# A convolution in two blocks of 128 tokens, and layernorm statistics on ScalarE, in the first stage of a fused attention and FFN kernel

## The chip, the cores and the metric

The kernel runs on one core of one Trainium2 chip. The metric is the device time of one execution in microseconds. A profile of one execution is kept beside the times; its span (first to last instruction) is longer than the times of the unprofiled runs.

## The reference, cut to what matters

Four blocks run one after the other on x of shape (8, 256, 256) (batch, token, channel): an attention block with a state space model, a routed tree FFN, a second attention and a mixture of experts. The change lies in the first block, except that the statistics of its result, which the second block needs, are taken inside the first stage too. For each batch, with `layernorm` written as LN:

```python
x_text = LN(x)                                   # the input statistics
scores = (x_text @ Wq) . (ctx @ Wk) / sqrt(32)   # 4 heads, 256 x 256
topv, topi = top_k(scores, 32); probs = softmax(topv)
attn_mean = mean over heads of probs at topi, 0 elsewhere
c_t = attn_mean @ (ctx @ Wv)
x1 = LN(x_text) * g + b, scaled and shifted by c_t @ W_film_in
y  = irfft(rfft(x1, n=512) * rfft(K, n=512))[:256] + x1 * D_skip   # causal convolution
y  = y scaled and shifted by c_t @ W_film_out
xt = x_text + y
h  = gelu(LN(xt) @ W1 + b1) @ W2 + b2
x  = x + LN(xt + h)                              # then the second block takes LN(x)
```

The convolution kernel K (256 channels x 256 taps) comes from exp(dt*A) of 64 states and is computed once, before the loop over batches.

## The kernel before, in words

The work of the first stage (`first_stage`) is laid out on 128 partitions: a batch of 256 tokens is ST = 2 tiles of 128 tokens. The transforms are real matrices of sines and cosines at 256 half-odd frequencies, applied by TensorE. The stage has a prologue, in which VectorE builds the tables of the state space model (from the start to about 87 us), TensorE turns them into K and its spectrum `kr`, `ki`, and the first batches are projected; and a loop that is written out as steps i = -1 to 9. A step works on four or five batches at once: m = i (attention average, modulation, convolution), b = i+1 (top-32 selection), f = i+2 (input norm, projections, scores), e = i-1 (second layernorm and the FFN's products), z = i-2 (output norm and result). Each engine has its own `step(i)`, a fixed order of instructions; engines wait for each other by semaphores.

- VectorE (`dve`): `xt` of e and its statistics (L820, L821), `xr` of z and its statistics, then for b the first eight maxima of each of R = 8 rows (4 heads x 2 tiles, `eight`, L773) and their removal (`take`, L783), `x1` of m (L849, L853), `x_stats(i + 3)` and `next_stats(i - 3)` (L754, L879), three more rounds of maxima, then L866 subtracts the row maximum from the 32 selected values, four of the last eight removals, `shares_of` (L793: sums of the exponentials), the other four removals, and `pairs_of` (L805, L808), whose result `pair` TensorE needs first in the next step (L1195).
- ScalarE (`act`): copies from PSUM, `exponents` (L609), the copies of the modulation (L686), four gelus (L598), the copy of the spectrum `spec` (L693), four more gelus, `projected` (L615, L619), `top_exponents` (one instruction, L623), `scaled_shares` (L631), `scores_out` (L639). An ACT_TABLE_LOAD stands before the first gelu and before the first exponential after a gelu.
- GpSimd (`pool`): per batch rstd and offsets from VectorE's statistics (`factors`, `next_factors`, `root`), two full-size additions and products for z, `xt_pre` (L502), and the product of the two spectra (L508 to L517).
- TensorE (`pe`): transposes of `pair` (L1195), context product (L1209), `film_in` and `film_out` tiles (L1097), the first four of eight `up` chunks (L1106), the forward transform (L1240: 8 matmuls of 256 columns), the other four chunks, transposes and projection of f (L1125) between the two halves of `down` (L1118), scores (L1142, L1144), and the inverse transform (L1278: 8 matmuls of 256 columns).

A matmul in float32 stands as two records in the profile. `up(e)` writes four PSUM slots in turn, so that chunks 4 to 7 wait for the gelus of chunks 0 to 3. After the loop the next stage begins behind a barrier of all engines.

## Time and profile before

| | us |
|---|---|
| median of 3 runs (lowest, highest) | 1381.75 (1381.48, 1383.94) |
| span of the profiled execution, all that is recorded of its time | 1503.4 |
| first stage in the profile: prologue | 0 to about 118 |
| starts of VectorE's steps 1 to 8 (L820) | 155.23, 192.53, 229.85, 267.38, 304.99, 342.29, 379.54, 413.71 |
| last instruction of the first stage (L839) | 446.02 |
| busy share of the whole span: TensorE, VectorE, ScalarE, GpSimd | 80%, 59%, 39%, 31% |

How to read it: times in the rows are microseconds from the start of the profiled execution, and means are in ns where marked. A row of the timeline merges like instructions that stand next to each other (x16) and says in brackets how long the engine had been idle and what ended that. The clock of a window is the share of TensorE's full clock that was granted: 1.00 is 2.4 GHz, 0.50 is 1.2 GHz, and a value between them is a window with both.

### The profile page before, as it was taken

How to read it: one execution, taken by the hardware profiler on the slowest of the kernel's cores; microseconds unless marked ns; L12 is line 12 of the kernel's file. 1: busy time of each engine (PE TensorE's matmuls, PEld its weight loads, DVE VectorE, ACT ScalarE, POOL GpSimd, SP SyncE). 2: the span in 40 equal slices, each digit the busy share in tenths (PEclk: the TensorE clock that was granted, in tenths of full speed). 3: DMA queues.
4: the chain of work that ended last, by engine and by line, in shares of the span. 5: the costliest groups of instructions: out<-in, count | busy, mean ns of one | idle time of the engine just before them, and what ended most of it. 6: DMA issues, size and time to landing. Idle time of an engine off the chain costs nothing. (4 is left out here: it accounts for less than half of the span.)

```text
span 1503.4 us, 24492 instructions
## 1 busy us (share of the span) xinstructions
PE 1203.0 (80%) x7028; PEld 869.8 (58%) x7032; DVE 887.9 (59%) x2553; ACT 580.3 (39%) x1116; POOL 466.2 (31%) x749
## 2 busy tenths in 40 slices
PE   2597999999857756584958793868999989999997
PEld 1395677777646545373746672655666645555554
DVE  8998999999234643452625363565766634453534
ACT  2324566665322113252635331634666641212110
POOL 2237344555450336326141704622221000000000
PEclk9858999999979978697978896876999999999999
DMA  9000000000007412383823731625100000000000
GB/s 267 0 2 1 1 1 1 1 1 1 1 8 192 143 43 80 107 252 97 262 80 91 259 101 56 96 70 136 16 13 10 2 1 1 14 0 14 0 14 15
DMA packets 92463, 91.98 MB, mean 61 GB/s; under 512 B 27057, under 2 KB 77747, under 8 KB 92341
## 3 DMA queue, kind: packets, MB, share of 16 engines
q1 hardware_dynamic: 80052, 65.32, 14.5%
q0 software_dynamic: 12288, 25.18, 6.8%
q8 instruction: 59, 0.97, 0.3%
q14 instruction: 64, 0.52, 0.1%
HBM read 75.79 MB, written 14.68 MB: 60 GB/s over the span
## 5 line engine op out<-in xcount | busy, mean ns | idle before, releaser
L2263 PE MATMUL gq_psH<-gq_xT,gq_w 128*128 (+1 forms) x564 | 102.9, 309 | 53.3 <-ACT gq_act L1981 28.4
L2263 PEld LDWEIGHTS gq_psH<-gq_xT,gq_w 128*128 128x128 f32 x564 | 83.4, 209 | 81.6 <-issue 76.6
L3503 ACT ACTIVATE m_silu<-m_psG 128x512 f32<-128x512 f32 x48 | 28.7, 597 | 215.3 <-PE m_psU L3623 215.3
L2273 PE MATMUL gq_psY<-leaf_w,gq_hT 128*128 (+1 forms) x282 | 95.2, 422 | 20.0 <-issue 14.3
L3556 DVE TENSOR_TENSOR m_act<-m_silu,m_psU 128x512 f32<-128x512 f32 x48 | 33.0, 687 | 122.5 <-ACT m_silu L3503 107.7
L1865 POOL DMA_INDIRECT gq_x<-rows_x,gq_token_i x48 | 47.0, 979 | 174.0 <-PE gq_psX L2252 105.6
L3623 PE MATMUL m_psG<-m_xnT,m_gate 128*128 128x512 f32 x192 | 91.2, 597 | 2.1 <-PEq L192 2.1
L3623 PE MATMUL m_psU<-m_xnT,m_up 128*128 128x512 f32 x192 | 91.4, 599 | 0.0
L2149 DVE SCALAR_TENSOR_TENSOR gq_hT<-gq_xT,unit_leaf,gq_act 128x128 f32<-128x128 f32 x141 | 49.6, 352 | 61.7 <-issue 28.6
L1981 ACT ACTIVATE gq_act<-gq_psH,leaf_b 128x128 f32<-128x128 f32 x141 | 51.4, 365 | 75.4 <-remote 41.5
L783 DVE MATCH_REPLACE8 s_product_a_rest<-a_top,s_product_a_rest 128x256 f32<-128x256 f32 x192 | 76.1, 408 | 0.3 <-issue 0.3
L3034 DVE TENSOR_REDUCE c_max<-c_psA 128x4 f32<-128x1024 f32 x32 | 39.2, 1226 | 61.3 <-PE c_psA L3185 61.3
L205 POOL TENSOR_SCALAR m_rstd<-m_mean_var 128x4 f32<-128x4 f32 x4 | 0.9, 232 | 229.8 <-DVE m_mean_var L1348 229.8
L2910 ACT ACTIVATE c_probT<-c_psA 128x2048 f32<-128x2048 f32 x32 | 60.1, 1878 | 28.5 <-PE c_psA L3216 28.5
L2168 DVE TENSOR_TENSOR gq_y<-gq_psY,gq_y 128x256 f32 (+1 forms) x94 | 39.7, 422 | 46.9 <-remote 29.0
L3635 PE MATMUL m_psD<-m_down,m_act 128*128 128x256 f32 x256 | 60.9, 381 | 7.1 <-DVE m_acc L3581 7.1
L3581 DVE SCALAR_TENSOR_TENSOR m_acc<-m_psD,m_weight,m_acc 128x256 f32<-128x256 f32 x128 | 53.1, 477 | 22.3 <-PE m_psD L3635 22.3
L773 DVE MAX8 a_top<-s_product_a_rest 128x8 f32<-128x256 f32 x192 | 64.9, 410 | 2.0 <-DVE s_product_a_rest L783 0.5
L3623 PEld LDWEIGHTS m_psU<-m_xnT,m_up 128*128 128x128 f32 x192 | 37.1, 193 | 46.8 <-issue 46.8
L1106 PE MATMUL a_psW<-s_tables_a_work,a_w 128*128 128x256 f32 x256 | 60.8, 393 | 2.7 <-ACT s_tables_a_work L675 2.7
L3635 PEld LDWEIGHTS m_psD<-m_down,m_act 128*128 128x128 f32 x256 | 48.1, 190 | 25.6 <-issue 14.2
L1657 PE MATMUL gq_psH<-rows_ahead,gq_xT 128*128 128x256 f32 (+1 forms) x192 | 53.9, 429 | 9.3 <-ACT rows_ahead L1564 7.8
(574 smaller groups left out, 3063.6 us busy)
## 6 DMA issues: line engine op xcount, KB each, us to landing
leaf_w<-in_group_w SPq DMA_DIRECT2D x128, 128.0 KB
leaf_w<-in_group_w SPq DMA_DIRECT2D x64, 256.0 KB
a_w<-in_L_xattn_W SPq DMA_DIRECT2D x2, 1024.0 KB, 11.9
rows_x<-token_rows SPq DMA_DIRECT2D x8, 256.0 KB, 5.4
sorted_y_q<-gq_y SPq DMA_DIRECT2D x16, 128.0 KB, 3.9
sorted_y_k<-rows_ahead SPq DMA_DIRECT2D x16, 128.0 KB, 4.4
sorted_y_v<-gq_y SPq DMA_DIRECT2D x16, 128.0 KB, 1.7
rows_f<-token_rows SPq DMA_DIRECT2D x8, 256.0 KB
```

The source lines that it names most:

```text
L773: do.mark(dve.max(top[:, j, 8 * r:8 * r + 8], row_in(r, j)))
L783: last = dve.match_replace(rest[:, j, :], top[:, j, 8 * r:8 * r + 8], row_in(r, j), NEG_TAKEN)
L1106: last = pe.matmul(pW[:, 2 + c // 2 % 2, c % 2, :], w1[:, k, c * P:(c + 1) * P], hT[:, k, :], start=(k == 0), stop=(k == DC - 1))
L1657: last = pe.matmul(self.psL[n % 2][0:k, c, :], self.nw[:, f, d, c * P:c * P + k], self.xnT[:, b, d, :], start=(d == 0), stop=(d == DC - 1))
L1981: act.activation(act_h[n % 2][:], psH[n % 2][:, 0:P], ACT.Gelu if gelu else ACT.Relu, bias=weights.b1[:, first + f, bass.ds(g, 1)]).then_i ...
L2149: dve.scalar_tensor_tensor(hT[n % 2][:], xT[:, DC, bass.ds(g * -P + u * P, P)], leaves.unit_leaf[:, bass.ds(g, 1)], act_h[n % 2][:], ALU.i ...
L2263: last = pe.matmul(psH[n % 2][:, 0:P], w1[n % 3][:, c, :], xT[:, c, bass.ds(g * -P + u * P, P)], start=(c == 0), stop=(c == DC - 1))
L2273: pe.matmul(psY[n % 3][:, 0:D], hT[n % 2][:], weights.w2[:, bass.ds(g * D, D)], start=True, stop=True).then_inc(y_ps, 1)
L2910: act.activation(probT[c][:], psA[:], ACT.Exp, scale=float(DH1) ** -0.5).then_inc(exps.s, 1)
L3581: last = dve.scalar_tensor_tensor(acc[:, t, :], psD[:, t, :], wt[:, t, e:e + 1], acc[:, t, :], ALU.mult, ALU.add)
L3623: last = pe.matmul(o[u % 2][:], w[:, u, c, :], xnT[:, c, :], start=(c == 0), stop=(c == DC - 1))
L3635: last = pe.matmul(psD[:, t, :], act_u[u % 2][:, t * P:(t + 1) * P], down[:, u, :], start=True, stop=True)
```

## The change

It does four things, all in the first stage.

1. Convolution by blocks. The 256 tokens are two blocks of 128, and the transform has 128 frequencies (every second row or column of the old tables; for the inverse, the first 128 rows of the table, every second column, copied by GpSimd once). Both blocks are transformed at once, by two matmuls of 512 columns. The kernel's spectrum is kept for its first 128 taps (`kr[:, 0]`, `ki[:, 0]`) and for taps 128 to 255 (`[:, 1]`); `shifted_spectrum` combines them once with a sign per frequency, so that the second block's result is its own product plus the first block's product with the combined one. GpSimd multiplies in `block_products`: 4 products and 2 sums of 512 columns, signalled as `y_first`, then 4 products, 2 sums and 2 additions of 256 columns, signalled as `y_sb`. The inverse has 2 matmuls of 256 columns for each token tile.
2. Order. TensorE's forward transform now stands before all eight `up` chunks, and ScalarE copies the spectrum before all eight gelus.
3. Statistics. Mean and variance of x are taken by ScalarE (`sums`, `squares`, each with an accumulating output, for tiles 0-1, 2-3 and 4-15), all in the prologue; the small factors follow on GpSimd in the same three groups. The next stage's statistics, one batch a step before, are taken by VectorE for batches 0 to 4 in step 7 behind `x1`, and for 5 and 6 in step 9; GpSimd's factors follow in `next_factors(0, 5)`, at the end of step 7, and `next_factors(5, 7)`, in step 9.
4. Top-32 exponentials. L866 goes. ScalarE takes exp(scale * top - scale * max) in 8 instructions of 32 columns with the bias from `nmax`, and its table is loaded as before ahead of the first.

```diff
 # loads: half-length tables, cut by the DMAs; the kernel's table in 16 DMAs into a blanked tile
-        load(dft[:], self.dram["dft"], self.late)
-        load(idft[:], self.dram["idft"], self.late)
+        even = self.dram["dft"].rearrange("(p two) t k f -> two t p k f", two=2)
+        for t in range(ST):
+            load(dft[t * P // ST:(t + 1) * P // ST], even[0, t, :, :, 0:P], self.late)
+        load(idft_in[:], self.dram["idft"][:, 0], self.late)
...
 # gpsimd, step(i)
-                    if ST <= i + 3 < B:
-                        factors(i + 3)
-                    if 0 <= i - 4 < NEXT - 2:
-                        next_factors(i - 4)
                     if has(m):
                         reached(pool, fout_sb, m)
                         pool.tensor_tensor(f_out[:, :, D:2 * D], f_out[:, :, D:2 * D],
                                            xn[m % SLOTS][:], ALU.add).then_inc(xt_pre.s, 1)
+                        if m == 0:
+                            shifted_spectrum()
                         reached(pool, spec_sb, m)
...
+                        block_products(m)
+                    if m == B - 1:
+                        next_factors(0, NEXT - 2)
...
+                def block_products(m):
...
+                    for n, (a, k) in enumerate(four):
+                        do.mark(pool.tensor_tensor(part[n], x[a], own[k], ALU.mult))
+                    released(pool, y_ps, m)
+                    do.wait()
+                    do(pool.tensor_tensor(y[0], part[0], part[1], ALU.subtract))
+                    pool.tensor_tensor(y[1], part[2], part[3], ALU.add).then_inc(y_first.s, 1)
+                    reached(pool, y_first, m)
+                    for n, (a, k) in enumerate(four):
+                        do.mark(pool.tensor_tensor(part[n][:, 0], x[a][:, 0], shifted[k], ALU.mult))
+                    do.wait()
+                    do.mark(pool.tensor_tensor(part[0][:, 0], part[0][:, 0], part[1][:, 0],
+                                               ALU.subtract))
+                    do(pool.tensor_tensor(part[2][:, 0], part[2][:, 0], part[3][:, 0], ALU.add))
+                    do(pool.tensor_tensor(y[0][:, 1], y[0][:, 1], part[0][:, 0], ALU.add))
+                    pool.tensor_tensor(y[1][:, 1], y[1][:, 1], part[2][:, 0], ALU.add
+                                       ).then_inc(y_sb.s, 1)
...
 # scalar
                 def top_exponents(b):
                     reached(act, ranked, b)
-                    act.activation(etop[:], etop[:], ACT.Exp, scale=scale
-                                   ).then_inc(etop_sb.s, 1)
+                    for j in range(R):
+                        last = act.activation(etop[:, j, :], top[:, j, :], ACT.Exp,
+                                              bias=nmax[:, j:j + 1], scale=scale)
+                    last.then_inc(etop_sb.s, 1)
...
-                    if has(e):
-                        gelus(e, range(HC // 2))
                     if has(m):
                         reached(act, spec_ps, m)
                         released(act, y_sb, m)
                         act.activation(spec[:], pW[:, 0:2].rearrange("p c k d -> p c (k d)"),
                                        ACT.Copy).then_inc(spec_sb.s, 1)
                     if has(e):
-                        gelus(e, range(HC // 2, HC))
+                        gelus(e, range(HC))
...
 # vector, step(i)
                     if z == B - 1:
-                        next_stats(NEXT - 1)
+                        next_stats(NEXT - 2, NEXT)
...
-                    if ST <= i + 3 < B:
-                        x_stats(i + 3)
-                    if 0 <= i - 3 < NEXT - 1:
-                        next_stats(i - 3)
+                    if m == B - 1:
+                        next_stats(0, NEXT - 2)
...
-                        dve.tensor_tensor(etop[:], top[:], top[:, :, 0].unsqueeze(2)
-                                          .to_broadcast([P, R, TOPK]), ALU.subtract
-                                          ).then_inc(ranked.s, 1)
+                        reached(dve, ranked, b)
...
 # tensor, step(i)
-                    if has(e):
-                        reached(pe, hT_sb, e)
-                        up(e, range(HC // 2))
                     if has(m):
                         reached(pe, x1_sb, m)
                         for part in range(2):
-                            for k in range(2):
-                                for t in range(ST):
-                                    last = pe.matmul(pW[:, part, k, :],
-                                                     dft[:, t, part, k * P:(k + 1) * P],
-                                                     x1[:, t, :], start=(t == 0),
-                                                     stop=(t == ST - 1))
+                            last = pe.matmul(flat(pW[:, part]), dft[:, part],
+                                             x1[:].rearrange("p t d -> p (t d)"), start=True,
+                                             stop=True)
                         last.then_inc(spec_ps.s, 1)
                     if has(e):
-                        up(e, range(HC // 2, HC))
+                        reached(pe, hT_sb, e)
+                        up(e, range(HC))
...
                         for t in range(ST):
+                            reached(pe, (y_first, y_sb)[t], m)
                             for part in range(2):
-                                for k in range(2):
-                                    last = pe.matmul(pA[:, t, :],
-                                                     idft[:, k, part, t * P:(t + 1) * P],
-                                                     yspec[:, part, k * D:(k + 1) * D],
-                                                     start=(part == 0 and k == 0),
-                                                     stop=(part == 1 and k == 1))
+                                last = pe.matmul(pA[:, t, :], idft[:, part],
+                                                 yspec[:, part, t * D:(t + 1) * D],
+                                                 start=(part == 0), stop=(part == 1))
```

## Rows read from the trace of the kernel before

**Rows 1.** The page's first line: the span of the profiled execution.

```profile
span 1503.4 us, 24492 instructions
```

**Rows 2.** Stage windows, 215 to 260 us: busy us (instructions) by engine, clock, DMA.

```profile
215.00:260.00 45.00, 43.23 (x219) 33.64 (x218) 42.95 (x156) 26.27 (x50) 24.74 (x34) 1.00 0.00 1
```

**Rows 3.** Timeline of loop step 5: start us, us, engine, line, operation [idle before].

```profile
304.99 0.68 DVE L820 TENSOR_TENSOR s_tables_a_work<-a_psA,s_tables_a_work 128x512 f32<-128x512 f32 x1
318.01 2.32 PE L1106 MATMUL a_psW<-s_tables_a_work,a_w 128*128 128x256 f32 x10
320.94 1.28 ACT L598 ACT_TABLE_LOAD   x1
321.47 3.62 PE L1240 MATMUL a_psW<-s_tables_a_work,a_dft 128*128 128x256 f32 x16
322.24 1.57 ACT L598 ACTIVATE s_tables_a_work<-a_psW,a_b 128x256 f32<-128x256 f32 x4
...
332.38 1.03 PE L1125 MATMUL a_psB<-a_xnT,a_wq 128*128 128x256 f32 x4
333.16 0.89 DVE L866 TENSOR_TENSOR s_dC_a_etop<-a_top 128x256 f32<-128x256 f32 x1
333.44 0.38 ACT L619 ACTIVATE a_qk<-a_psB 128x256 f32<-128x256 f32 x1 [3.54 <-PE a_psB L1125]
335.14 0.42 ACT L623 ACTIVATE s_dC_a_etop<-s_dC_a_etop 128x256 f32<-128x256 f32 x1
335.59 0.42 DVE L793 TENSOR_REDUCE a_einv<-s_dC_a_etop 128x8 f32<-128x256 f32 x1
...
342.29 0.68 DVE L820 TENSOR_TENSOR s_tables_a_work<-a_psA,s_tables_a_work 128x512 f32<-128x512 f32 x1
342.52 2.02 PE L1195 MATMUL a_psW<-identity,s_Z_re_a_pair 128*128 128x128 f32 x16 [0.68 <-DVE s_Z_re_a_pair L808]
```

**Rows 4.** Timeline, VectorE: the two sets of statistics in step 3; where step 4 starts.

```profile
241.62 0.75 DVE L754 BATCH_NORM_STATS2 a_x_stats<-x_tokens 128x6 f32<-128x256 f32 x2
...
243.63 2.68 DVE L773 MAX8 a_top<-s_product_a_rest 128x8 f32<-128x256 f32 x8
...
267.38 0.68 DVE L820 TENSOR_TENSOR s_tables_a_work<-a_psA,s_tables_a_work 128x512 f32<-128x512 f32 x1
```

**Rows 5.** Groups by form, ScalarE: busy us, mean ns of one | idle before.

```profile
L609 ACT ACTIVATE s_product_a_prob<-a_score,a_nmax 128x256 f32<-128x256 f32 x64 | 26.4, 501 | 24.4 <-DVE a_nmax L776 24.4
...
L3496 ACT ACTIVATE m_score<-m_score 128x32 f32<-128x32 f32 x4 | 0.9, 229 | 0.9 <-DVE m_score L3516 0.9
```

**Rows 6.** Timeline, TensorE: matmuls that end pauses of 2.69, 3.33 and 3.34 us.

```profile
51.91 0.66 PE L1054 MATMUL a_psA<-identity,a_xn 128*128 128x128 f32 x4 [2.69 <-ACT a_xn L590]
...
379.76 0.46 PE L1195 MATMUL a_psW<-identity,s_Z_re_a_pair 128*128 128x128 f32 x2 [3.33 <-DVE s_Z_re_a_pair L808]
...
856.84 1.11 PE L2613 MATMUL t_psY<-identity,token_rows 128*128 128x128 f32 x4 [3.34 <-issue]
```

**Rows 7.** Stage windows around those pauses, and after the restart at 147.14 us.

```profile
51.00:57.00 6.00, 4.41 (x14) 3.45 (x15) 5.55 (x18) 2.19 (x5) 0.00 (x0) 0.73 0.01 3
377.00:383.00 6.00, 2.50 (x18) 2.27 (x19) 5.52 (x10) 0.62 (x2) 0.59 (x2) 1.00 0.00 0
855.00:861.00 6.00, 3.01 (x16) 2.54 (x16) 1.73 (x4) 1.28 (x2) 4.82 (x10) 0.57 0.57 127
...
147.00:152.00 5.00, 4.86 (x12) 3.89 (x13) 4.66 (x21) 3.00 (x8) 0.09 (x1) 0.50 0.00 0
```

**Rows 8.** Groups by form, GpSimd: busy us, mean ns of one | idle before.

```profile
L508 POOL TENSOR_TENSOR s_tables_a_work<-s_tables_a_work,kernel_re 128x512 f32<-128x512 f32 x8 | 10.2, 1271 | 24.2 <-ACT s_tables_a_work L693 24.2
...
L206 POOL TENSOR_TENSOR a_next_hold<-a_next_hold,minus_half 128x2 f32<-128x2 f32 x7 | 5.0, 710 | 0.6
...
L206 POOL TENSOR_TENSOR m_rstd<-m_rstd,m_minus_half 128x4 f32<-128x4 f32 x4 | 4.1, 1032 | 0.3
```

**Rows 9.** Timeline, GpSimd: the first factor of the last batch's second layernorm.

```profile
416.51 0.22 POOL L205 TENSOR_SCALAR a_rstd<-a_mean_var 128x2 f32<-128x2 f32 x1 [7.98 <-DVE a_mean_var L757]
```

More of the change, by code:

```diff
@@ L372, in has, with tiles_of @@
             return 0 <= n < B
+        def tiles_of(group):
+            return slice(*(ST * b for b in ((0, 1), (1, 2), (2, B))[group]))
         STEPS = range(-2, B + 2)
@@ L428, in film_gains, with next_factors @@
+                def next_factors(first, end):
+                    reached_apart(pool, n_var, end - 1)
+                    q = slice(first * ST, end * ST)
+                    n = q.stop - q.start
+                    do(standard_factors(core, pool, do, tokens.factor[:, q], n_hold[:, 0:n],
+                                        tokens.mv[:, q, 1], [h[:, 0:n] for h in n_half]))
                 def film_gains():
@@ L485, in step @@
                             biased.then_inc(last_biased, 1)
[L486 to L487 removed]
+                            next_factors(NEXT - 2, NEXT)
                         released(pool, o_sb, z)
@@ L534, in _ @@
                 pool.tensor_copy(neg_mask[:], neg_mask[:]).then_inc(picked, 1)
-                factors(0)
-                factors(1)
+                for n, value in enumerate((-0.5, 0.5)):
+                    do(pool.memset(n_half[n][:], value))
+                for group in range(3):
+                    centres(group)
+                    factors(group)
                 pool.wait_ge(tables, 2)
@@ L719, in _ @@
                 projected(0)
+                act.wait_ge(core.loads[0], 16)
+                sums(1)
                 scores_out(0)
+                squares(1)
                 film_folded()
-                act.wait_ge(core.loads[0], 16)
                 x_normal(1)
@@ L727, in _ @@
                     keys_out(n)
+                sums(2)
+                squares(2)
                 exponents(0)
```

184 lines of the change are left out of this document (117 added, 67 removed).

## The prediction

> **What bounds the kernel now.** I read first the windows over the loop, then the timeline of one step, then who ends each wait. In the loop TensorE is busy 43.2 of 45 us and VectorE 43.0, at full clock [rows 2]: neither alone sets the pace. Step 5 shows how they share it. VectorE starts it at 304.99 and the next at 342.29, 37.30 us later [rows 3]. Counted from the start: TensorE begins the first `up` chunks at 13.02, the projection ends in ScalarE's copy at 28.45, behind that stands a table load of 1.28, the exponential of the 32 selected values starts at 30.15, and VectorE's `shares_of` starts at 30.60, at once after its end (30.57). VectorE itself would have been ready earlier: L866 starts at 28.17, and 0.43 for it and 1.6 for four removals (0.4 each) give 30.2. So in a step with one set of statistics the chain TensorE, `projected`, table load, exponential sets `shares_of`, and everything behind it (6.70 us to the next start) hangs on that. Step 4, which has two sets, takes 37.61 (267.38 to 304.99) [rows 3, 4]: 1.0 us more of VectorE's work stretched it by only 0.31. VectorE's chain and the other one are within half a microsecond of each other. Shortening one alone is worth little.
>
> **The change, part by part, in one loop step with all its parts (steps 1 to 5).**
> VectorE loses one or two sets of statistics, 2.01 for two [rows 4], so 1.0 each, and L866 at 0.43 (0.89 where it meets GpSimd [rows 3]). It would be ready for `shares_of` at about 28.7.
> TensorE: 256 columns are two records of 0.216, 0.43 per matmul, from 16 records in 3.46 (321.47 less 318.01). The forward transform falls from 8 matmuls to 2 of 512 columns, 3.46 to 1.73; the inverse from 8 to 4, also 3.46 to 1.73. But the forward one now stands ahead of all `up` chunks, and these wait on gelus. From 13.02: transform to 14.75, chunks 0 to 3 to 18.21. ScalarE is done with its copies at 15.95 (where the load stands, 320.94), copies the spectrum for 1.02, loads the table for 1.28 (18.25), and two gelus of 0.37 to 0.47 end at 19.09 [rows 3]. Chunk 4 waits for them, so TensorE stands for 0.95 us; its last chunk ends at 22.65 where it ended at 23.40. Of 1.73 us it gains 0.75 before the projection (bounds 0.4, were the handshakes slower, and 1.73 without the stall). `x1` is ready before the transform needs it (in step 3, which starts at 229.85, VectorE is through with it at 241.62 [rows 4], 11.8 into the step) and costs nothing.
> ScalarE: one instruction of 0.42 becomes eight of 32 columns with a bias from a tile. None such is in the trace. The nearest: 32 columns without such a bias take 229 ns, 256 columns with it 501 ns [rows 5] and without it 0.42 [rows 3]. So the bias costs 0.08 and one of the eight takes 0.31. In a row they start before the last has ended, the 256-column ones by 0.10 (64 of them are 26.4 us busy, 0.41 each, for a mean of 501 ns [rows 5]), which leaves 0.21: 7 x 0.21 + 0.31 = 1.78, bounds 1.2 and 2.5 (eight times 0.31, no overlap). That is 1.36 more, on the chain that sets `shares_of`.
> Together `shares_of` starts at 30.60 - 0.75 + 1.36 = 31.2, 0.6 later than now, and VectorE, ready at 28.7, waits for it 2.5 us. Steps 1 to 5 take 37.9 each, 189.5 for 187.1 now: +2.4. The other four removals and `pairs_of` follow as before.
> GpSimd: 4 products and 2 sums of 512 columns at 1.27, 1.23 apart [rows 8], are 7.6 as before; the 8 operations of 256 columns add 6.0 at about 0.7 (bounds 0.64, half of 1.27, and 1.27). It starts behind the copy of the spectrum at 17.0, so `y_sb` is up at 30.6; TensorE comes to the second half of the inverse at 33.3. Hidden, with 2.7 to spare; at 1.27 per operation 2 us would stick out of it.
>
> **Prologue and step 0.** There VectorE paces nearly all. It loses two sets (1.0 each) and L866, and half of a third set (its first one hid partly behind ScalarE's sines), and gains 0.3 for two small operations on one column: -1.1 to the tables, -2.5 to the end of step -1, where 0.9 is given back because `top_exponents` stands before ScalarE's copy of the kernel. Step 0 loses a set and L866 and keeps VectorE as its pace. Step 1 then starts 1.95 earlier (bounds 1 and 3). ScalarE takes 16 sums and 16 squares, at 0.5 and perhaps 0.2 more for reading the accumulator. The 24 of the last group, some 17 us, have ScalarE's longest idle stretch to themselves, 24.4 us before the first L609 [rows 5]; were it gone, every one would push step -1 by 0.7. The 8 others stand in shorter idle stretches. The 16 small DMAs of the kernel's table are last in SP's queue and needed only after all of VectorE's tables; all the loads move fewer bytes.
>
> **Steps 6 and 7 and the end.** Step 6 has no projection, so the exponentials start when the maxima are done: 1.8 us less. Step 7 waits for the convolution alone: transform from 13.0, spectrum at 16.0, `y_first` at 23.6, `y_sb` at 29.6, inverse to 30.75, where it is now 34.2. But GpSimd, before it takes the layernorm factors of the last batch, now runs `next_factors(0, 5)` on 10 columns. A power on 2 columns is 0.71 and on 4 is 1.03 [rows 8], 0.16 a column, so 2.0 for 10. The factors of one batch, three powers, six small operations of 0.2 and their waits, are 4.3; on 10 columns 8.2 (bounds 4.3, were a power's time fixed, and 13, were it proportional). It ends at 37.8, and the factors that now start at 416.51, 36.97 into the step [rows 9] (step 7 starts 0.22 before the matmul at 379.76 [rows 6]), start 0.9 later. Up to here the sum is -1.95 + 2.4 - 1.8 + 0.9 = -0.5: nothing.
>
> **TensorE's clock.** Now 0.68 us pass between the last inverse matmul and the next step's first matmul [rows 3]. After the change it is 0.68 + 0.75 (it is earlier) + 1.73 (shorter inverse) + 0.6 (`pair` is later) = 3.76 us in every step. What such a pause does is in the trace. Seven pauses of 2.69 to 3.37 us began at full clock; six were followed by half clock. The first (clock 0.73 in 51 to 57), the last (0.57 in 855 to 861) and the one that kept 1.00, of 3.33 at 379.76, stand in [rows 6, 7]. All eight longer ones that began so were followed by half clock. So I take it that nearly every step begins at 1.2 GHz. What that costs: matmuls take twice as long until the clock returns, and after the pause that ended at 147.14 it was still at 0.50 five microseconds on [rows 7]. The step's beginning (transposes 2.0, context product 1.9, `film_in` 3.4) is broken by two copies, and lies on the path to the projection. I take 3.3 us a step (bounds 0 and 5.7, all of it up to most of `film_in` at half speed). 1.0 of this comes back, since the stall at chunk 4 goes when TensorE is late: 2.3 net. Step 1 2.5, steps 2 to 5 9.2, step 6 2.3, and step 7, with no stall to lose, 3.3: +17.3. The pause does not heal, because both its ends hang on the same projection.
> The Trainium skill, TensorE: Matmul & The Clock Gate, section "HAM oscillation — how this bites in real kernels", says that waits between short bursts send the array back to half rate each time, so that each burst starts cold. The trace agrees in 14 of its 15 pauses of over 2.6 us; by the rule the sum is the +17 above, by the one row that held it is about 0.
>
> **Sum.** -0.5 + 17.3 = +16.8 us on the profiled execution's span of 1503.4 [rows 1], the only time it has. The median of the runs is 1381.75, 121.65 less; the stage moves almost no data, so I carry the difference over one to one: 1398.6. In proportion it would be 15.4.
>
> **Rivals.**
> Clock holds (0.22): pauses come out shorter or the steps' phase spares them. For it: the pause of 3.33 that held, and an exponential nearer 1.2 us would leave 3.2. Against it: six of seven. The parts cancel: 1381, from 1376 (no stall at chunk 4, 1 us off in each of five steps) to 1387 (two steps of seven start cold).
> VectorE is the pace after all (0.16), and the time goes below that of before: the eight exponentials hide, `shares_of` starts at about 28.7, which needs the projection 1.5 us earlier and the exponentials at 0.1 us each. Steps 1 to 5 then save 1.9 to 2.2 each, and with -1.95, -1.8 and +0.9 the time is 1369. It decides as soon as the chain through ScalarE ends before VectorE's fourth removal. Against it: step 4 stretched by only 0.31 for 1.0 of VectorE's work.
> Slower by more than the forecast (0.06): GpSimd's 256-column operations take 1.0 or more and push the inverse, or the powers grow faster than 0.16 a column: 1407 and above.
>
> **How the numbers follow.** Forecast 0.56, with a range of its own from 1389 to 1406. The 8 in 10 range goes from 1374, which leaves most of the VectorE rival out, to 1407. A difference of 0.2% is 2.8 us. Slower by more than that: forecast 0.56, the last rival 0.06 and 0.06 of the clock rival, 0.68. Within: 0.11 of the clock rival, with 0.01 of the others, 0.12. Faster: 0.16 and 0.04 of the clock rival, 0.20.
>
> **What would show it.** Steps 1 to 5 of 39 to 42 us, clock below 1.00 in most of them, pauses before L1195's successor of 3.4 us or more; eight exponentials in 1.6 to 2.0; VectorE idle before `shares_of`; TensorE idle about 1 us inside the `up` chunks in steps that start warm; a gap of 4 us between `next_stats`' factors and the last layernorm. Full clock through the loop, or `shares_of` starting before 29.5, would make it wrong.

## The result, and the profile after

The changed kernel takes 1389.53 us in the median of 8 runs (1382.60 to 1399.45), the kernel before 1382.85 beside it: ratio 1.0068, 95% interval 1.0043 to 1.0094, in which one slow run of the kernel before, 1622.98, does not count. Run again later in 12 runs, unaltered, it took 1387.20 (1382.03 to 1399.54) against 1381.30: 1.0047, 1.0024 to 1.0071. So it is slower, by 6 to 7 us between the medians, where 16.8 was forecast; the sign, the mechanism and the range held, and the size was off by more than a factor of two.

One thing has to be known to read the profiles. The profiled execution of the changed kernel is its slowest, 1399.45, and its first stage (to the start of the last sum into x) ends at 463.29 us. In the kernel before that is 446.02, so there the stage is 17.3 us longer. The profiled execution of the later 12 ends it at 458.06. From that point to the end of the span the profiled executions of all kernels with the unchanged rest need 925 to 937 us, the unusual one of the kernel before excepted (1057). Stages are therefore compared by the trace, kernels by their medians.

The windows of the changed kernel's steps 1 to 7, from one of VectorE's starts (L916, the L820 of before) to the next; columns: window, its length, busy us (instructions) of TensorE, its weight loads, VectorE, ScalarE, GpSimd, the granted clock, DMA (the first line is the profile page's own):

```profile
span 1397.7 us, 24202 instructions
...
153.96:193.59 39.63, 34.37 (x158) 25.02 (x158) 32.06 (x113) 23.25 (x49) 15.76 (x19) 0.93 0.00 1
193.59:233.75 40.16, 34.91 (x158) 25.37 (x158) 33.63 (x118) 24.24 (x51) 20.87 (x26) 0.92 0.00 1
233.75:273.06 39.31, 33.75 (x158) 24.49 (x158) 33.63 (x118) 24.13 (x51) 20.87 (x26) 0.96 0.00 1
273.06:312.21 39.15, 33.90 (x158) 24.36 (x158) 33.61 (x118) 24.24 (x51) 20.88 (x26) 0.95 0.00 1
312.21:351.55 39.34, 33.77 (x158) 24.52 (x158) 33.62 (x119) 24.13 (x51) 20.89 (x26) 0.96 0.00 1
351.55:392.46 40.91, 35.20 (x122) 23.46 (x122) 34.17 (x118) 20.25 (x45) 20.87 (x26) 0.83 0.00 1
392.46:428.19 35.73, 33.50 (x122) 22.93 (x122) 9.56 (x36) 10.91 (x20) 22.53 (x28) 0.86 0.00 1
```

The reader is to see that no step has full clock, and that TensorE and VectorE are busy for only 34 of 39 us where it was 43 of 45 us [rows 2]: the change made both lighter and the loop slower. Step 5 of it, in a timeline, shows why; it answers to [rows 3], with the rows picked out that matter here:

```profile
312.21 0.68 DVE L916 TENSOR_TENSOR s_tables_a_work<-a_psA,s_tables_a_work 128x512 f32<-128x512 f32 x1
312.44 3.44 PE L1285 MATMUL a_psW<-identity,s_Z_re_a_pair 128*128 128x128 f32 x16 [3.79 <-DVE s_Z_re_a_pair L904]
326.66 1.88 PE L1325 MATMUL a_psW<-s_tables_a_work,a_dft 128*128 128x512 f32 x4
332.68 3.72 PE L1196 MATMUL a_psW<-s_tables_a_work,a_w 128*128 128x256 f32 x16 [0.68 <-ACT s_tables_a_work L685]
341.31 0.38 ACT L706 ACTIVATE a_qk<-a_psB 128x256 f32<-128x256 f32 x1 [3.54 <-PE a_psB L1215]
341.71 1.28 ACT L711 ACT_TABLE_LOAD   x1
343.00 1.80 ACT L711 ACTIVATE s_dC_a_etop<-a_top,a_nmax 128x32 f32<-128x32 f32 x8
344.84 0.42 DVE L889 TENSOR_REDUCE a_einv<-s_dC_a_etop 128x8 f32<-128x256 f32 x1 [3.61 <-ACT s_dC_a_etop L711]
345.98 2.00 PE L1364 MATMUL a_psA<-s_tables_a_work,a_idft 128*128 128x256 f32 x8
351.55 0.68 DVE L916 TENSOR_TENSOR s_tables_a_work<-a_psA,s_tables_a_work 128x512 f32<-128x512 f32 x1
351.78 2.67 PE L1285 MATMUL a_psW<-identity,s_Z_re_a_pair 128*128 128x128 f32 x16 [3.80 <-DVE s_Z_re_a_pair L904]
```

TensorE waits 3.79 us for `pair`; VectorE waits 3.61 us for the eight exponentials; they wait for the copy of the projection, and that waits for TensorE. The two engines wait for each other in turn. The 16 transposes behind the pause take 3.44 us, and 2.02 at full clock [rows 3].

### The profile page after: what moved, and what is told of

Its sections match the earlier page's. It is cut to its first block and busy times, and to the rows that moved or that the text cites. A ratio compares the mean times of both kernels' runs of the same rounds, so it can differ in the third digit from the quotient of the medians.

```text
span 1397.7 us, 24202 instructions
## 1 busy us (share of the span) xinstructions
PE 1174.1 (84%) x6872; PEld 835.4 (60%) x6872; DVE 877.6 (63%) x2515; ACT 610.2 (44%) x1242; POOL 497.2 (36%) x732
## 5 line engine op out<-in xcount | busy, mean ns | idle before, releaser
L2348 PE MATMUL gq_psH<-gq_xT,gq_w 128*128 (+1 forms) x564 | 98.8, 300 | 4.8 <-ACT gq_w L2058 2.6
L2348 PEld LDWEIGHTS gq_psH<-gq_xT,gq_w 128*128 128x128 f32 x564 | 78.8, 199 | 30.6 <-issue 25.9
L2358 PE MATMUL gq_psY<-leaf_w,gq_hT 128*128 (+1 forms) x282 | 89.5, 401 | 7.2 <-DVE gq_hT L2234 6.9
L2066 ACT ACTIVATE gq_act<-gq_psH,leaf_b 128x128 f32<-128x128 f32 x141 | 51.3, 364 | 37.9 <-PE gq_psH L2348 23.7
L3720 PEld LDWEIGHTS m_psD<-m_down,m_act 128*128 128x128 f32 x256 | 48.1, 190 | 25.6 <-issue 14.2
L1196 PEld LDWEIGHTS a_psW<-s_tables_a_work,a_w 128*128 128x128 f32 x256 | 49.2, 195 | 20.1 <-ACT s_tables_a_work L685 7.3
L2058 ACT ACTIVATE gq_w<-leaf_w 128x256 f32 (+1 forms) x141 | 58.3, 414 | 3.8 <-issue 3.7
```

Of the source, the lines that this page charges most:

```text
L1196: last = pe.matmul(pW[:, 2 + c // 2 % 2, c % 2, :], w1[:, k, c * P:(c + 1) * P], hT[:, k, :], start=(k == 0), stop=(k == DC - 1))
L2058: act.activation(w1[n % 3][:], weights.w1[:, :, bass.ds(g * P, P)], ACT.Copy).then_inc(w_sb, 1)
L2066: act.activation(act_h[n % 2][:], psH[n % 2][:, 0:P], ACT.Gelu if gelu else ACT.Relu, bias=weights.b1[:, first + f, bass.ds(g, 1)]).then_i ...
L2348: last = pe.matmul(psH[n % 2][:, 0:P], w1[n % 3][:, c, :], xT[:, c, bass.ds(g * -P + u * P, P)], start=(c == 0), stop=(c == DC - 1))
L2358: pe.matmul(psY[n % 3][:, 0:D], hT[n % 2][:], weights.w2[:, bass.ds(g * D, D)], start=True, stop=True).then_inc(y_ps, 1)
L3720: last = pe.matmul(psD[:, t, :], act_u[u % 2][:, t * P:(t + 1) * P], down[:, u, :], start=True, stop=True)
```

## The experiments

All were timed in five rounds against the kernel before, whose median was 1381.3 us (beside experiment 8: 1379.9). Each differs from the kernel named by its edit alone, of which the core is quoted. Each expectation sets two theories, A and B, against each other.

**1. The clock alone.** Changed kernel, TensorE kept busy in its pauses.

```diff
 # tensor, step(i), behind the inverse transform
+                    if 1 <= m <= B - 2:
+                        reached(pe, fout_sb, m)
+                        for _ in range(4):
+                            pe.matmul(flat(pC[:]), w1[:, 0, 0:P], w1[:, 0, 0:2 * S], start=True, stop=True)
```

> The changed kernel with four matmuls of 512 columns of which nothing is kept, issued by TensorE behind the inverse transform of batches 1 to 6, where it pauses for 3.8 us (3.45 us of work at full clock). Theory A (the pauses bring the half clock and that costs time): full clock from step 1 to step 6; the half-clock stretches at 192, 233, 274, 312, 353 and 394 us go; shares_of starts 31.2 to 31.6 us into a step instead of 32.6, steps of 38.1 us instead of 39.3; 6 to 10 us less than the changed kernel, 1380 to 1384, and a narrower spread of its runs. Theory B (the loop is slower by the exponentials alone, TensorE's half clock is covered by waits): no difference, 1389.

Measured: 1381.78, ratio 0.9986 (0.9962 to 1.0010). Its windows of steps 2, 5, 6 and 7:

```profile
194.42:232.33 37.91, 35.78 (x166) 24.60 (x166) 33.53 (x118) 24.25 (x51) 20.89 (x26) 1.00 0.00 1
...
308.17:346.08 37.91, 35.78 (x166) 24.61 (x166) 33.53 (x119) 24.25 (x51) 20.89 (x26) 1.00 0.00 1
346.08:381.92 35.84, 32.73 (x130) 22.33 (x130) 33.64 (x119) 20.36 (x45) 20.91 (x26) 1.00 0.00 1
381.92:413.44 31.52, 29.30 (x122) 20.80 (x122) 9.55 (x36) 11.02 (x20) 22.53 (x28) 1.00 0.00 1
```

TensorE has 3.5 us more work at full clock in each step, and steps 2 to 5 are 1.2 to 2.4 us shorter. Theory A. Without the half clock the change can't be told from the kernel before. 1387.20 less 1381.78 makes the clock 5.4 us in the medians; the two ratios, 1.0047 and 0.9986, make it 8.4, so its size is known only roughly.

**2. One exponential for the eight.** Changed kernel with VectorE's subtraction and ScalarE's single instruction of 256 columns put back.

```diff
 # scalar, top_exponents
-                    for j in range(R):
-                        last = act.activation(etop[:, j, :], top[:, j, :], ACT.Exp, bias=nmax[:, j:j + 1], scale=scale)
+                    act.activation(etop[:], etop[:], ACT.Exp, scale=scale)
```

> The changed kernel with VectorE's subtraction and the single exponential of 256 columns as before, all else changed. Theory A (ScalarE's chain of projection, table load and exponentials sets shares_of): 1.38 us less in each of steps 1 to 5, 0.43 more in steps -1 and 0, so -6; TensorE's pauses shrink from 3.8 to 2.4 us. If half clock still follows them 1383; if it does not, 1375 to 1378. Theory B (VectorE is the pace, or GpSimd's y_sb): 0 to +3, 1389 to 1392.

Measured: 1378.69, ratio 0.9980 (0.9962 to 0.9998), 8.5 us less than the changed kernel. The loss goes this way too, since the eight exponentials are what makes the pauses long. Steps with full clock take 36.5 to 37.0 us, and `shares_of` starts at 29.8 in them. The pauses are 2.40 to 2.90 us, and after three of five of them the clock stayed. The first of these rows held, the second fell (timeline of TensorE, then the windows from there):

```profile
192.58 2.02 PE L1284 MATMUL a_psW<-identity,s_Z_re_a_pair 128*128 128x128 f32 x16 [2.88 <-DVE s_Z_re_a_pair L899]
...
266.12 3.65 PE L1284 MATMUL a_psW<-identity,s_Z_re_a_pair 128*128 128x128 f32 x16 [2.88 <-DVE s_Z_re_a_pair L899]
...
192.00:197.00 5.00, 4.02 (x28) 3.43 (x28) 4.58 (x14) 0.98 (x2) 1.61 (x5) 1.00 0.00 0
265.00:271.00 6.00, 4.48 (x23) 4.25 (x24) 5.58 (x15) 1.12 (x3) 2.07 (x5) 0.72 0.02 4
```

**3. The eight exponentials on the kernel before**, and no other part of the change.

```diff
 # vector: behind the last maxima
-                        dve.tensor_tensor(etop[:], top[:], ..., ALU.subtract).then_inc(ranked.s, 1)
 # scalar, top_exponents
-                    act.activation(etop[:], etop[:], ACT.Exp, scale=scale)
+                    for j in range(R):
+                        last = act.activation(etop[:, j, :], top[:, j, :], ACT.Exp, bias=nmax[:, j:j + 1], scale=scale)
```

> The kernel before with only its exponentials of the selected values changed: no subtraction on VectorE, eight instructions of 32 columns on ScalarE. Theory A: the eight take 1.8 us for 0.42, shares_of starts 1.4 us later in each of steps 1 to 5 (31.9 to 32.0 us into a step), 0.43 us less in steps -1 and 0; TensorE's pause becomes 2.1 us and the clock stays; +6, 1387 to 1390. Theory B (VectorE is the pace of the kernel before): 0.4 less per step, 1379 to 1381.

Measured: 1390.04, ratio 1.0052 (1.0027 to 1.0078): 8.7 us more, the same as their price in the changed kernel. `shares_of` starts at 31.99 to 32.00 in steps with full clock, and after two of the five pauses of 2.07 us at the ends of steps 1 to 5 half clock followed, which the expectation had excluded. ScalarE and VectorE in step 4, which starts at 272.96 and has full clock:

```profile
301.83 1.28 ACT L624 ACT_TABLE_LOAD   x1
303.12 1.81 ACT L624 ACTIVATE s_dC_a_etop<-a_top,a_nmax 128x32 f32<-128x32 f32 x8
304.96 0.42 DVE L799 TENSOR_REDUCE a_einv<-s_dC_a_etop 128x8 f32<-128x256 f32 x1 [1.16 <-ACT s_dC_a_etop L624]
```

**4. The exponentials off the path.** Changed kernel, eight exponentials ahead of the copy of the projection.

```diff
 # scalar, projected(f): between the copy of xnT and the copy of the projection
+                    act.activation(warm[:], nmax[:, 0:1], ACT.Exp, scale=scale)   # loads the table
+                    top_exponents(b)
                     reached(act, proj_ps, f)
```

> The changed kernel with ScalarE's eight exponentials of the selected values ahead of the copy of the projection, and the table asked for by an exponential of one column that waits for nothing. Theory A (both ends of TensorE's pause hang on the chain projection, table load, exponentials): that chain leaves shares_of, which starts when VectorE's removals end, 29.0 to 29.4 us into a step instead of 32.6; the pause at the end of a step shrinks to under 1 us; full clock through the loop; steps 1 to 5 of 35.7 to 36.5 us; 1362 to 1370. Theory B (the exponentials only wait for VectorE's last maxima, and the copy of the projection, now behind them, delays the scores and with them TensorE): steps of 38 us or more, 1380 to 1389.

Measured: 1370.68, ratio 0.9909 (0.9876 to 0.9943) in 6 runs, just over the expected range; theory A, though the pause did not fall under 1 us as expected. Step 4 of it, ScalarE, VectorE and the end:

```profile
284.06 1.28 ACT L712 ACT_TABLE_LOAD   x1
285.36 0.20 ACT L712 ACTIVATE a_warm<-a_nmax 128x1 f32<-128x1 f32 x1
286.75 1.81 ACT L717 ACTIVATE s_dC_a_etop<-a_top,a_nmax 128x32 f32<-128x32 f32 x8 [1.19 <-DVE a_top L876]
288.46 0.36 ACT L709 ACTIVATE a_qk<-a_psB 128x256 f32<-128x256 f32 x1
288.58 0.42 DVE L900 TENSOR_REDUCE a_einv<-s_dC_a_etop 128x8 f32<-128x256 f32 x1 [0.17 <-ACT s_dC_a_etop L717]
...
295.51 2.02 PE L1296 MATMUL a_psW<-identity,s_Z_re_a_pair 128*128 128x128 f32 x16 [1.26 <-DVE s_Z_re_a_pair L915]
```

VectorE waits 0.17 us, not 3.61, and TensorE 1.26, not 3.79. The clock stays at full in steps 1 to 6, and steps 2 to 4 take 35.4 to 35.5. Nothing was made faster: 16 us of the changed kernel's median went by the order of two waits on ScalarE.

**5. The same order in the kernel before.**

```diff
 # scalar, projected(f): before the wait for the projection
+                    act.activation(warm[:], nmax[:, 0:1], ACT.Exp, scale=scale)
+                    top_exponents(b)                                              # one instruction
```

> The kernel before with its one exponential of the selected values, and its table load, ahead of the copy of the projection; all else as before. Theory A (in the kernel before, VectorE's own chain is half a microsecond behind the chain through ScalarE): shares_of starts at 30.2 us into a step with one set of statistics instead of 30.6, and at 31.2 in one with two sets; 2 us less in all, 1378 to 1381. Theory B (the chain through ScalarE was the only limit): shares_of at 29, 1372 or less.

Measured: 1380.79, ratio 1.0005 (0.9987 to 1.0022). Steps 1 to 5 take 36.89, 36.80, 37.51, 37.60 and 37.26 where they took 37.30, 37.32, 37.53, 37.61 and 37.30 [rows 3, 4]. Theory A: the kernel before had VectorE's chain right behind the other, so the order alone is worth 1 us there in all five, and the medians can't be told apart. The slack that experiment 4 uses is what the change made.

**6. The changed kernel once more.**

```diff
 # no line differs
```

> The changed kernel itself, unaltered, beside the others of this job. Theory A (each step starts behind a pause of 3.8 us and at half clock, and how long the half clock lasts after it differs from one execution to the next): pauses of 3.8 us again, half-clock stretches at other places and of other lengths than in the first profile, runs spread over more than 8 us, median 1386 to 1391. Theory B (the cost per step is fixed): runs within 4 us of each other.

Measured: 1387.20, runs from 1382.03 to 1399.54. Six pauses of 3.75 to 3.80, all followed by half clock again, for 3.4 us four times and for 6.8 twice; in the first profile it was 3.4 three times, and 6.8, 13.7 and 10.2. So the length differs between executions, as theory A has it. The spread of the times, 17 us, proves less than I expected of it: the kernel before ranges over 11 beside it and over 15 in all runs of the experiments (1373.88 to 1389.49), and it had full clock in its loop in the one execution that was profiled.

**7. The stall at chunk 4, first try.** Experiment 1 with the transform and the copy of the spectrum back between the two halves of `up` and of the gelus.

```diff
 # tensor, step(i), in all steps; ScalarE's gelus and copy likewise
+                        up(e, range(HC // 2))
                     ... # forward transform
-                        up(e, range(HC))
+                        up(e, range(HC // 2, HC))
```

> The changed kernel with the four filling matmuls of 512 columns behind the inverse transform (nothing of them is kept), and with the forward transform and the copy of the spectrum back in the middle of the up chunks and of the gelus. Theory A (TensorE stands for 0.7 to 1.0 us at chunk 4 because the transform went ahead, and that lies on the path to the projection): the stall goes, shares_of starts at 30.3 instead of 31.2 us into a step, 0.9 us less in each of steps 1 to 5, 1376 to 1379. Theory B (GpSimd's product, whose spectrum now comes 2 us later, holds the inverse transform back, 34 us or more into a step): steps as long as with the filling alone or longer, 1381 or more.

Measured: 1387.90, ratio 1.0036 (1.0023 to 1.0049): a miss. The stall went, but `y_sb` came 34.1 us into the step and the filling matmuls then held the next step's transposes back by 0.65 us, so that steps 2 to 5 took 37.6 to 37.9 where they took 37.9. The loss is in step 7, which took 39.65 us instead of 31.52. In step 6 TensorE waits 5.14 us for `y_sb`, the clock falls in that wait, and the inverse and the filling matmuls (5.05 us for 3.60 at full clock) run on until 4.65 us into step 7; the rest comes from the convolution, which alone is the path there.

**8. The stall, second try.** No filling, the old order in steps 1 to 5 alone.

```diff
 # tensor, step(i); ScalarE's gelus and copy likewise
+                    if has(e) and has(f):
+                        reached(pe, hT_sb, e)
+                        up(e, range(HC // 2))
                     ... # forward transform
-                        up(e, range(HC))
+                        up(e, range(HC // 2 if has(f) else 0, HC))
```

> The changed kernel with the forward transform and the copy of the spectrum back in the middle of the up chunks and of the gelus in steps 1 to 5, and ahead of them in steps 6 and 7; no filling. Theory A (the stall at chunk 4 lies on the path to the projection, and the kernel with filling and the old order lost its gain because GpSimd's y_sb at 34 us pushed the filling matmuls over the start of the next step, and at steps 6 and 7, where the convolution alone is the path): shares_of starts at 30.2 to 30.5 us into a step, steps of 36.9 to 37.3 us, TensorE waits about 1 us inside the inverse transform for y_sb, its pause at the end of a step is 1.8 to 2.2 us, and the half clock goes from most of steps 1 to 5; 1376 to 1382. Theory B (y_sb holds back the step itself): steps of 38 us or more, 1385 or more.

Measured: 1386.44, ratio 1.0035 (1.0012 to 1.0057): another miss. The mechanism was there (no stall, TensorE waits 0.90 to 1.22 us for `y_sb` inside the inverse), the gain not: five pauses of 2.62 us, and half clock after all five. Step 4 begins:

```profile
310.83 3.33 PE L1287 MATMUL a_psW<-identity,s_Z_re_a_pair 128*128 128x128 f32 x16 [2.62 <-DVE s_Z_re_a_pair L906]
...
310.60:349.00 38.40, 34.09 (x158) 24.51 (x158) 33.87 (x119) 24.28 (x51) 20.93 (x26) 0.95 0.00 1
```

Where the half clock lasts 3.4 us such a step takes 38.4 to 38.7 us, for 39.1 to 39.4 in the changed kernel, so the stall does lie on the path and is worth 0.4 to 1.0; but two of the five had 6.8 us of half clock (39.44 and 39.70), and the medians of the two kernels, each over its own base, can't be told apart. I had expected a pause of about 2 and full clock.

**9. The first two parts alone**: the changed kernel with all statistics on VectorE and the single exponential.

```diff
 # vector, step(i), behind x1; its prologue, GpSimd's factors and ScalarE's sums and squares likewise
+                    if ST <= i + 3 < B:
+                        x_stats(i + 3)
+                    if 0 <= i - 3 < NEXT - 1:
+                        next_stats(i - 3)
-                    if m == B - 1:
-                        next_stats(0, NEXT - 2)
```

> The kernel before with the first two parts of the change alone: convolution by blocks, transform and copy of the spectrum ahead. VectorE takes all statistics and the subtraction, ScalarE one exponential of 256 columns, as before. Theory A (two chains: through ScalarE shares_of could start at 29.8 us, but VectorE is ready at 30.2 with one set of statistics and at 31.2 with two): steps of 36.9 and 37.9 us, pauses of TensorE of 2.4 to 3.2 us with half clock behind some of them, no delay of the last batch's layernorm factors on GpSimd; 1378 to 1383. Theory B (VectorE's statistics hide): steps of 36.5 us, 1373 to 1377.

Measured: 1392.06, ratio 1.0063 (1.0040 to 1.0086): a miss for both theories, by 9 us. The place is step 0. GpSimd there, then TensorE and VectorE (timeline):

```profile
114.41 0.22 POOL L205 TENSOR_SCALAR a_x_rstd<-a_x_mean_var 128x2 f32<-128x2 f32 x1
120.45 0.52 POOL L1493 MEMSET leaf_path<- 128x512 bf16 x1
121.12 12.73 POOL L1500 TENSOR_SCALAR_AFFINE_SELECT leaf_path<-leaf_path 128x128 bf16<-128x128 bf16 x18
...
145.08 1.27 POOL L524 TENSOR_TENSOR s_tables_a_work<-s_tables_a_work,kernel_re 128x512 f32<-128x512 f32 x1
154.59 3.37 POOL L531 TENSOR_TENSOR s_tables_a_work<-s_tables_a_work,kernel_im 128x256 f32<-128x256 f32 x2
...
161.77 2.07 PE L1367 MATMUL a_psA<-s_tables_a_work,a_idft 128*128 128x256 f32 x4 [6.62 <-POOL s_tables_a_work L537]
163.88 0.69 DVE L906 TENSOR_TENSOR s_tables_a_work<-a_psA,s_tables_a_work 128x512 f32<-128x512 f32 x1 [6.51 <-PE a_psA L1367]
```

The factors of two batches of x (from 114.41 to 120.45, and 3.1 us from 138.04) stand ahead of the product of the spectra, which takes 16.6 us here (145.08 to 161.7), 14.5 in the changed kernel and took 7.8 in the kernel before. TensorE waits for it and VectorE for TensorE, and step 1 starts at 163.88 instead of 153.96. In the changed kernel GpSimd is through with all factors of x at 90.3. The same queue also holds work that this stage does not need: `leaf_path` and the other tables of the routed FFN take GpSimd 17.5 us here (120.45 to 137.95) and 20.1 in the changed kernel (113.00 to 133.14), ahead of the product in all these kernels. No run moves them.

**10. Statistics back on VectorE in experiment 4.**

```diff
 # experiment 4, and with it
+                        x_stats(i + 3)                 # as in experiment 9, with GpSimd's factors
+                        next_stats(i - 3)
```

> The changed kernel with the exponentials and their table ahead of the copy of the projection, and with the statistics of x and of the next stage back on VectorE, batch by batch, as before. Theory A (once the exponentials are off the end of the chain, VectorE is the pace, so each set of statistics counts in full): 1.0 us more per set, 36.4 us for steps with one set and 37.4 with two, 7 sets in steps 1 to 5; 2 us more in the prologue, 4 us less at the end, where GpSimd's factors of 10 columns are gone; 1374 to 1379. Theory B (they hide): steps of 35.4 us, 1364 to 1368.

Measured: 1391.45, ratio 1.0064 (1.0037 to 1.0091). Step 1 starts at 164.38, the same cause; steps 2 and 3 take 36.85 and 38.30 where they took 35.50 and 35.38, so one and two sets cost 1.35 and 2.92, half clock in the second included. Theory A in the loop, and its sum missed step 0.

**11. GpSimd's factors in the last step.** Experiment 4 and:

```diff
 # gpsimd: end of step 7, and step 9
-                    if m == B - 1:
-                        next_factors(0, NEXT - 2)
...
-                            next_factors(NEXT - 2, NEXT)
+                            next_factors(0, NEXT)
```

> The changed kernel with the exponentials and their table ahead of the copy of the projection, and with GpSimd's factors of the next stage for batches 0 to 6 in one go on 14 columns in the last step, not for 0 to 4 on 10 columns in step 7. Theory A (those on 10 columns, 8.5 us, delay the last batch's layernorm factors by 4.2 us, and that delays the end of the stage): 4 us less than the same without it, 1364 to 1368. Theory B (the delay is hidden, or the 14 columns now stick out at the end): 1369 to 1372.

Measured: 1365.65, ratio 0.9881 (0.9867 to 0.9895). The last batch's layernorm factors start 2.80 us after VectorE's last step does (404.62 less 401.82), and 6.86 in experiment 4. From the start of that last step to the end of the stage it is 32.13 for 36.16. Theory A; the intervals of the two medians overlap, the 4 us are read from the traces.

**12. The version that beats both.** Experiment 11 with filling matmuls in the three long pauses left: five behind the inverse of batch 6, six ahead of the last transposes of h and three behind them.

```diff
 # tensor, step(i); fill(n): n matmuls as in experiment 1
+                    if m == B - 2:
+                        fill(5)                        # behind the inverse
...
+                    if e == B - 1:
+                        fill(6)                        # ahead of the transposes of h
                         transposes(pA, h).then_inc(hT_ps.s, 1)
+                        fill(3)
```

> The changed kernel with the exponentials and their table ahead of the copy of the projection, GpSimd's factors of the next stage in the last step, and matmuls of 512 columns of which nothing is kept in TensorE's three long pauses: five behind the inverse of batch 6, six ahead of the last transposes of h, three behind them. Theory A (half clock after these pauses lies on the path: up and down of the last batch run alone): step 7 1.3 us shorter, the last up in 6.4 us instead of 9.1, down at full clock; 4 to 6 us less than without them, 1359 to 1362. Theory B (these stretches wait for something else): 1364 to 1366.

Measured: 1362.01, ratio 0.9862 (0.9833 to 0.9890), 19 us below the kernel before. Against experiment 11 it is 3.6 us in the medians, with intervals that overlap, so no gain is shown in the time. In the traces it is there: the last `up` is shorter (first row: experiment 11, second: this), and the stage ends 4.9 us earlier (429.08 for 433.96), of which 0.6 was there before the first filling matmul.

```profile
411.25 9.94 PE L1205 MATMUL a_psW<-s_tables_a_work,a_w 128*128 128x256 f32 x32 [2.71 <-ACT s_tables_a_work L768]
```

```profile
409.13 7.17 PE L1205 MATMUL a_psW<-s_tables_a_work,a_w 128*128 128x256 f32 x32 [0.60 <-ACT s_tables_a_work L768]
```

## Why the prediction came out as it did

**The chain through ScalarE sets the loop.** Right. The eight exponentials took 1.80 us for an estimate of 1.78, one of them 306 ns for 0.31. At full clock `shares_of` started at 31.20 to 31.22 into the step for 31.2, and steps 2 to 5 took 37.91 to 37.93 for 37.9 (experiment 1). VectorE's wait of 2.5 was 2.71.

**VectorE as the pace (0.16).** It fell, by evidence from both sides: undoing the saving of 0.43 gained 8.5 us in experiment 2, and in experiment 4, where the chain was taken off, VectorE became the pace and the time fell to 1371. The rival of slower GpSimd work (0.06) fell too: 0.73 us for an operation of 256 columns in the loop.

**The sum without the clock, -0.5.** Measured +0.5 (medians, experiment 1 against the kernel before, interval of the ratio 0.9962 to 1.0010); its stage ends 3.1 us later in the trace (449.10 for 446.02), and 1.5 of that is step 1, which there too begins at half clock (39.44 for 37.91). The other parts: step 6 took 1.4 us less for 1.8 (35.84 for 37.25); step 7 with the tail +0.7 for +0.9, namely -2.65 in step 7 and +3.35 behind it, since GpSimd's factors on 10 columns held the last layernorm back:

```profile
426.79 1.98 POOL L206 TENSOR_TENSOR token_factor<-token_factor,a_next_minus_half 128x10 f32<-128x10 f32 x1
...
434.72 0.21 POOL L1401 TENSOR_TENSOR token_factor<-token_factor,a_next_hold 128x10 f32<-128x10 f32 x1
435.02 0.23 POOL L205 TENSOR_SCALAR a_rstd<-a_mean_var 128x2 f32<-128x2 f32 x1
```

They took 8.5 us for 8.2, the power 1.98 for 2.0. The traces of experiments 4 and 11 show the 4 us that the delay is worth by itself.

**The prologue, -1.95.** Too much. Step 1 started at 153.96 and 155.44 in the two executions, for 155.23 before: -1.3 and +0.2. "Step 0 ... keeps VectorE as its pace" was true by a narrow margin only, and for a reason that the prediction didn't give. The second half of the inverse there waits for GpSimd:

```profile
150.11 1.59 POOL L538 TENSOR_TENSOR s_tables_a_work<-s_tables_a_work 128x256 f32<-128x256 f32 x1
151.75 2.08 PE L1364 MATMUL a_psA<-s_tables_a_work,a_idft 128*128 128x256 f32 x4 [4.67 <-POOL s_tables_a_work L538]
153.96 0.68 DVE L916 TENSOR_TENSOR s_tables_a_work<-a_psA,s_tables_a_work 128x512 f32<-128x512 f32 x1
```

The inverse is through hardly before VectorE asks for it. The third part of the change is what kept it in time: it takes two sets of factors, 9.1 us, out of GpSimd's queue ahead of this product. The prediction counted GpSimd for the loop (0.73 us per operation of 256 columns for 0.7) and not for step 0, so it valued that part at 2 us. Between experiments 9 and 2, which differ in that part over the whole stage, it is 13.4, and 9.8 us of it are there when step 1 starts (163.88 and 154.10). By medians, taken in this order: parts one and two alone +10.8, part three -13.4, part four +8.5, together +5.9.

**The pauses.** Right: 3.76 forecast, 3.76 to 3.80 in six, 3.75 to 3.80 in the other six, and half clock after all twelve. The rival in which the clock holds (0.22) fell in both executions that were profiled. The forecast counted eight pauses longer than 3.37 that began at full clock; the trace of the kernel before has twelve, and half clock came with all of them.

**The price of a cold start** (a step that begins at half clock)**: the step that failed.** The prediction took 3.3 us a step (bounds 0 and 5.7), of which 1.0 was to come back, 2.3 net. Steps 2 to 7 lost 15.6 us against experiment 1 in the first profiled execution and 9.8 in the second, and between the medians it is 5.4 in all (8.4 by the ratios). No execution near the median was profiled, so how its loss is spread over the steps is not known. In the loop a half-clock stretch of 3.4 us cost 1.2 to 1.5, one of 6.8 cost 2.3 and 2.4 (40.16 and 40.34 for 37.91); only where it lasted over 10 us, as in steps 6 and 7 of the first execution, did it cost 5.1 and 4.2. Windows around the starts of steps 2 and 3, and in step 6, of the changed kernel:

```profile
192.00:200.00 8.00, 6.09 (x26) 5.41 (x27) 7.55 (x20) 1.93 (x3) 3.20 (x7) 0.57 0.00 0
233.00:237.00 4.00, 3.02 (x14) 3.05 (x15) 3.70 (x8) 0.00 (x0) 0.38 (x2) 0.57 0.00 0
237.00:241.00 4.00, 2.92 (x17) 2.02 (x16) 3.85 (x15) 1.87 (x4) 3.50 (x8) 1.00 0.00 0
353.00:367.00 14.00, 12.59 (x28) 6.45 (x27) 8.73 (x35) 3.15 (x6) 6.48 (x11) 0.51 0.00 1
```

At step 3 the clock is back before 237, when TensorE has done little more than the transposes: 1.4 us for 3.3. Nor did 1.0 of it come back: TensorE waits at chunk 4 for 0.68 to 0.70 us in steps 2 to 5 of both executions, as it does at full clock (0.68 in experiment 1), because the gelus are late as well. I had taken the clock's return from one row, five microseconds still at 0.50 behind the pause that ended at 147.14 [rows 7], and that pause had been 6.68 long, with the clock at 0.50 for its last 4.6 us. The bounds 0 and 5.7 were right; I chose by the one row I had, at the high end. The Trainium skill, TensorE: Matmul & The Clock Gate, section "HAM oscillation — how this bites in real kernels", says each burst behind such a wait starts cold. For these twelve pauses the trace agrees; how long a burst stays cold decided the size here. Over steps 2 to 5 the two executions agree (6.3 and 6.4 us lost against experiment 1, for 9.2 forecast); in steps 6 and 7 they do not (9.3 and 3.5, for 5.6).

**Carrying it over.** The sum was laid against the profiled execution and carried one to one to the median. The profiled execution showed +17.3 at the end of the stage, so the forecast met that execution and missed the median. Meeting it was luck, in which errors cancel: against experiment 1 the clock's part was 14.2 for 17.3, and the part without the clock was +3.1 in the trace for -0.5. Within the clock's part steps 2 to 5 lost 2.9 us less than forecast and steps 6 and 7 3.7 more, and the profiled execution was the slowest of eight.

## What to carry to other kernels

When two engines wait for each other once per step, look at what stands between the two waits on the third engine: here a table load and eight small exponentials stood behind a copy that they did not need, and moving them ahead was worth 16 us, where the whole change had cost 6. Work taken off engines that are not late becomes a pause, and a pause of TensorE may have a price of its own; measure it by filling the pause with work that nobody needs. Count the queue of every engine in the first and last iterations as well as in the steady loop: the 9 us of GpSimd's factors and the 4 us of its powers were both there.

## What was not expected of the hardware

The same pause does not always do the same. Of five pauses of 2.07 us two were followed by half clock (experiment 3), of five of 2.40 to 2.90 two (experiment 2), of five of 2.62 all five (experiment 8), of twelve of 3.75 to 3.80 all twelve. Yet a pause of 3.33 kept full clock in the kernel before [rows 6, 7] and again at the same place in experiment 5. So the length alone does not decide. What differs between 192.58 and 266.12 in experiment 2, both 2.88, no run tells. Half clock after them lasted from 3.4 to 13.7 us.

A GpSimd operation of 256 columns takes 0.73 us and one of 512 takes 1.27 in the loop, so splitting is not free; in step 0 some of the small ones took 1.59 and 1.69 (150.11 in the changed kernel, 3.37 for two in experiment 9), more than twice as long. They overlap VectorE's operations of 1024 columns (149.64 to 152.78 in the changed kernel, 152.08 to 157.37 in experiment 9); that these hold them up is read from the overlap, no run tests it.
